# One ScalarE instruction for the square roots of two places, with GpSimd's pieces in the first

## The reference

```python
q2 = jnp.sum(q * q, axis=-1)
k2 = jnp.sum(k * k, axis=-1)
qk = jnp.einsum('bhid,bhjd->bhij', q, k)
d2 = jnp.maximum(q2[..., :, None] + k2[..., None, :] - 2.0 * qk, 1e-12)
attn = jax.nn.softmax(-jnp.sqrt(d2), axis=-1)
out = jnp.einsum('bhij,bhjd->bhid', attn, v)
```

## Time and profile before

| | us |
|---|---|
| median of three runs | 1473.09 |
| the profiled execution | 1471.27 |
| its span, first to last instruction | 1469.5 |
| ScalarE busy | 1431.2 (97%) |
| VectorE busy | 1224.0 (83%) |
| TensorE matmul busy | 1119.0 (76%) |
| GpSimd busy | 833.3 (57%) |
| exponentials of layer 0 (L830), 63 | 438.9 |
| roots of layer 0 in whole places (L791), 59 | 388.1 |
| exponentials of layer 1 (L1349), 438 | 432.6 |

### The profile page before, as it was taken

The page is one execution under the profiler, slowest core; times in us unless marked ns, Lnnn a source line. Parts: engine busy times, 40 slices in busy tenths (PEclk is TensorE's granted clock), DMA queues, the critical chain, the costliest instruction groups (busy, mean ns, idle before and its releaser), DMA issues.

```text
span 1469.5 us, 22500 instructions
## 1 busy us (share of the span) xinstructions
PE 1119.0 (76%) x8231; PEld 471.7 (32%) x8260; DVE 1224.0 (83%) x2196; ACT 1431.2 (97%) x796; POOL 833.3 (57%) x737
## 2 busy tenths in 40 slices
PE   5588786887887988879878784787777677776766
PEld 2133234253452552534515321232223122221212
DVE  6988978978979779779697799858898898997886
ACT  3999999999999999999999999999999999999998
POOL 5178899768778787797887885633213033023100
PEclk8588988999999989899899997899999999999999
DMA  4942644222232234254352521033033033021020
GB/s 118 251 134 65 175 130 127 53 58 75 77 89 66 63 105 140 69 155 112 90 157 57 129 69 30 20 120 82 27 127 70 27 113 82 29 103 33 27 70 16
DMA packets 113185, 130.04 MB, mean 88 GB/s; under 512 B 42906, under 2 KB 81178, under 8 KB 113066
## 3 DMA queue, kind: packets, MB, share of 16 engines
q1 hardware_dynamic: 107738, 116.74, 29.0%
q0 software_dynamic: 4464, 11.09, 2.8%
q10 hardware_dynamic: 864, 0.69, 0.2%
HBM read 83.79 MB, written 44.70 MB: 87 GB/s over the span
## 4 chain that ended last, share of the span: by engine, by line
ACT 29%; PE 24%; DVE 23%; issue 17%; POOL 4%; DMA 1%; SPq 1%; DVEq 0%; ACTq 0%; POOLq 0%
DVE scores L737 15%; ACT exp L1349 11%; PE pvb L718 8%; ACT scores L830 8%; ACT scores L791 7%; PE ring L703 5%; PE ring L1059 5%; DVE exp L1357 4%; PE ring L1070 3%; ACT exp L1345 2%; POOL yro L1136 1%; PE ring L1324 1%; PE ring L480 1%; DMA w<-in_w 1%; ACT L830 0%
## 5 line engine op out<-in xcount | busy, mean ns | idle before, releaser
L737 DVE TENSOR_SCALAR scores<-ring 128x1024 f32<-128x1024 f32 x512 | 588.7, 1212 | 14.9 <-PE ring L703 14.7
L830 ACT ACTIVATE scores<-scores 128x8192 f32<-128x8192 f32 x63 | 438.9, 7021 | 0.2
L1349 ACT ACTIVATE exp<-ring 128x1024 f32<-128x1024 f32 x438 | 432.6, 1418 | 0.2
L1324 PE MATMUL ring<-stk 128*128 128x512 bf16 x995 | 299.9, 385 | 127.9 <-ACT exp L1349 106.2
L791 ACT ACTIVATE scores<-scores 128x7296 f32<-128x7296 f32 (+2 forms) x59 | 388.1, 6641 | 8.1 <-DVE scores L737 7.9
L1357 DVE SCALAR_TENSOR_TENSOR exp<-exp 128x512 f32<-128x512 f32 x438 | 322.2, 757 | 62.5 <-ACT exp L1349 58.2
L718 PE MATMUL pvb<-scores,val 128*9 128x256 f32 x4096 | 325.6, 393 | 61.4 <-issue 34.2
L703 PE MATMUL ring<-stk 64*128 64x512 bf16 x1024 | 210.2, 408 | 67.5 <-DVE scores L737 56.7
L1324 PEld LDWEIGHTS ring<-stk 128*128 128x128 bf16 x1024 | 65.8, 97 | 337.9 <-ACT exp L1349 241.7
L703 PEld LDWEIGHTS ring<-stk 64*128 64x128 bf16 x1024 | 49.8, 93 | 303.2 <-DVE scores L737 215.3
L718 PEld LDWEIGHTS pvb<-scores,val 128*9 128x9 f32 x4096 | 65.3, 89 | 184.8 <-issue 181.1
(11 more groups left out here) (263 smaller groups left out, 1482.0 us busy)
## 6 DMA issues: line engine op xcount, KB each, us to landing
stk<-stack SPq DMA_DIRECT2D x192, 192.0 KB, 2.9
w<-in_w SPq DMA_DIRECT2D x39, 352.0 KB, 3.4
w<-in_w SPq DMA_DIRECT2D x39, 192.0 KB, 2.9
stack<-qp SPq DMA_DIRECT2D x7, 768.0 KB, 4.4
stack<-kp SPq DMA_DIRECT2D x7, 768.0 KB, 5.7
xj<-xg SPq DMA_DIRECT2D x10, 448.0 KB, 4.7
yg<-xj POOLq DMA_DIRECT2D x10, 448.0 KB, 3.7
stack<-qp SPq DMA_DIRECT2D x7, 512.0 KB, 5.1
```

Source lines behind the costliest of these rows:

```text
L737: nc.vector.tensor_scalar(S[place][:, j * N:(j + 1) * N], tile, 1e-12, None, ALU.max).then_inc(o.release(("qk", group, place, j)), 1)
L830: nc.scalar.activation(S[place][:], S[place][:], ACT.Exp, scale=-1.0).then_inc(exp_done, 1)
L1324: mm = nc.tensor.matmul(out[:, cols], stk1[place][:, Q, i * P:(i + 1) * P], stk1[place][:, K, cols], start=True, stop=True)
L1349: nc.scalar.activation(EX[k // 2][:, k % 2, :], tile, ACT.Exp, scale=SCALE1).then_inc(o.release(("qk1", n, i)), 1)
```

## The change

- The tiles of places 0 and 1 are allocated as one tile `S01` of 16384 columns; `S[0]` and `S[1]` are its halves.
- From round 3 on (`PAIRED_FROM`), ScalarE takes the roots of places 0 and 1 by one instruction, over the columns of `S01` from the end of place 0's pieces to the end of place 1. It waits for the last chunk of place 1, and counts `root_done` up by 2.
- From round 3 on, GpSimd's pieces of place 1 are pieces of place 0, in the same widths.

```diff
-    ((), (896,), (448, 448), (448,)),
-    ((), (896,), (), ()),
-    ((), (448, 448), (), ()),
-    ((), (896,), (448, 448), ()),
...
-    ((), (448, 448), (448, 448), ()),
-    ((), (448, 448), (448,), ()),
+    ((896,), (), (448, 448), (448,)),
+    ((896,), (), (), ()),
+    ((448, 448), (), (), ()),
+    ((896,), (), (448, 448), ()),
...
+    ((448, 448), (), (448, 448), ()),
+    ((448, 448), (), (448,), ()),
 ]
...
-        S = [scores(f"scores{i}", [P, CH * N]) for i in range(GROUP - 1)]
+        S01 = scores("scores01", [P, 2 * CH * N])
+        S = [S01[:, 0:CH * N], S01[:, CH * N:2 * CH * N], scores("scores2", [P, CH * N])]
...
+        def act_root_pair(act, o, group):
+
+            o.emptied(act, ("qk", group, 1, CH - 1))
+            part = S01[:, columns_by_pool(group, 0):2 * CH * N]
+            nc.scalar.activation(part, part, ACT.Sqrt).then_inc(root_done, 2)
...
+        PAIRED_FROM = FIRST_JOBS
...
-                        for place in range(GROUP):
+                        if r >= PAIRED_FROM:
+                            act_root_pair(act, o, r)
+                        for place in range(2 if r >= PAIRED_FROM else 0, GROUP):
                             act_root_halves(act, o, r, place) if (r, place) == (1, GROUP - 1) else act_root(act, o, r, place)
...
                         for place in range(1, GROUP - 1):
-                            pool_roots(pool, o, roots, r, 1, place - 1, place)
+                            pool_roots(pool, o, roots, r, 0, place - 1, place)
...
                     if r > 1 and r != PLACE_ROUND + 1:
-                        pool_roots(pool, o, roots, r, 1)
+                        pool_roots(pool, o, roots, r, 1 if r < PAIRED_FROM else 0)
```

## The result

The changed kernel takes 1478.18 us (median of 15 runs, 1474.55 to 1480.70), the kernel before 1474.69 (15 runs, 1472.44 to 1476.42). The ratio is 1.0025, 95% interval 1.0018 to 1.0033: 3.7 us slower, with an interval from 2.7 to 4.9. The median of the kernel before over 15 runs is itself 1.6 us above that of the three runs of the prediction. The profiled execution of the changed kernel took 1480.70 us, the slowest of its 15.

What follows compares the result with a forecast made beforehand. ScalarE, busy 97% of the span, was taken as the bound. Round 4's +0.43, rounds 5 to 15's 11 x -0.096 = -1.06 and round 3's 0 gave -0.63 us: 1472.5 us from a 1473.09 median, range 1469.5 to 1475.8.

Steps and rivals of the forecast that it cites:

- Added: First root waits for place 1's last tile instead of place 0's; only round 4 late, by 4.19 us, costing 0.43 us.
- rival (a): ScalarE's wait stands ahead of the table load, which no longer hides it: +1.5 us, 1474.6 us; chance 0.10.
- a root with one wait like the pair: Evidence against the wait preceding the load: at 29.78 ScalarE loaded the table, then its first root stood 5.03 us.
- 0.43+1.28: Round 4 if the wait precedes the load: late pair's 0.43 us plus 1.28 us of load, +1.71 us.
- The joint: Cost between two back-to-back ScalarE roots, saved by the long root: 0.096 us a round, bounds 0 and 0.204.
- met by the 1.7 us that ScalarE is then behind: Round 13 if the wait precedes the load: ScalarE's lag covers the missing margin, so no added cost.
- +0.22: Round 14 if the wait precedes the load: 1.28 us needed against a margin of 1.06, adding 0.22 us.
- +0.65 less 0.10: Round 15 if the wait precedes the load: adds 0.65 us; the saved instruction is worth 0.096 us a round.
- the 6.65 us of cover: Round 4: GpSimd's piece ends at 302.65, exponential 0 starts at 309.30, so the new need costs nothing.
- the 0.11 us from mark to root: A stalled ScalarE root starts 0.11 us after VectorE's mark of a place's end; used to work out margins.
- the length of the long root: ScalarE's joined root in rounds 3 to 15: 128x15488, at some 13.1 us.
- the +5.7 us: Wait ahead of the load, with the skill's 1380 ns drain also behind it: +5.7 us, 1478.8 us; chance 0.01.

Runs made afterwards that it cites:

- one count: Changed kernel with the pair adding one to root_done instead of two, exponentials' waits adjusted: 1474.05 us, ratio 0.9999 to the kernel before.
- two counts: Kernel before, roots still single, but place 0's root adds two to root_done from round 3 on: 1473.01 us, ratio 0.9997.
- the two late roots: Changed kernel with two roots in place of the long one, both behind place 1, one count each: 1473.75 us, ratio 1.0003 to the kernel before.
- the pair with later gathers: Changed kernel with root_done raised by one per pair and round 14's gathers moved behind GpSimd's root pieces: 1471.99 us, ratio 0.9992 to the kernel before.

## Why the prediction was wrong

**The step that failed: "Added".** The prediction took the margin of a pair against the start of the root. That holds only if the load stands ahead of the wait. It gave rival (a) 0.10 because of the earlier trace rows, a root with one wait like the pair. The two differ in what they signal: that root signals nothing, the pair counts two. With a count of two the wait became an instruction of its own, and the table load was put between it and the root; with one count, the wait stayed on the root. The diff showed the two, and no root of the kernel before counts by two. The row was the wrong analogue, and the chance too small.

**The size of rival (a), +1.5 us for 3.7.** Its steps against the runs:

- Round 4: the step 0.43+1.28 = +1.71; measured 28.44-26.67 = +1.77. Rival (a) had this step right.
- The joint: 0.096 us a round; measured 0.09. The 13 long roots average 13.12 us, as forecast.
- Round 13: forecast 0, "met by the 1.7 us that ScalarE is then behind". Measured: a round of 59.85 us (load of round 12 to load of round 13) against 58.68 before, +1.2. The marks of place 1 are not independent of ScalarE there. In rounds 7 to 9 they stand 4.47 us ahead of the root in the kernels before and after alike, as TensorE is released by ScalarE's first exponential; so ScalarE's lag of round 4 had passed into the marks, and only the slack shrinks from there to round 13. The margin of the earlier trace rows was 1.19 us, under 1.28 by itself, and the joints of rounds 10 to 13 bring ScalarE 0.4 us nearer. The chain from place 1 of round 9 to that of round 13 also took 238.7 us in both profiles of the changed kernel; it took 237.9 and 237.7 in the two of the kernel before, and 238.7 in that with two counts, so this part belongs to the execution and not to the change. From the mark of round 9 to the end of round 13's exponentials the changed kernel takes 295.1 us in both profiles, and the one-count kernel and the two profiles of the kernel before 294.3.
- Round 14: forecast +0.22, since the row had place 1 ready 1.06 us ahead. Where round 14 is unpaired and the hole stands in place 1, three profiles have it 2 to 4 us late for place 0's root. Behind the mark of place 1 the roots then end 898.34-871.67 = 26.67 us later, in the one-count kernel too; in the changed kernel 902.60-874.92 = 27.68: +1.0 for the load.
- Round 15: forecast +0.65 less 0.10; measured, from one load for the exponentials to the next, 57.74-57.10 = +0.6.

With round 13's +1.2, round 14's +1.0 and round 15's +0.6, less 8 x 0.09 for rounds 5 to 12, the sum is +3.9 us against the 3.7 measured. The steps come from one or two profiles each, so the nearness of the sums is in part luck.

**What stays open: TensorE ahead of round 14.** In the second profile of the changed kernel TensorE waits 2.33 us before its first value product of round 14, and then its granted clock falls to the lower of its two levels (near 0.5 of 2.4 GHz) for some 3 us. Place 0 of round 14 ends 20.50 us behind ScalarE's load for the exponentials of round 13. The rows, and the stretch behind the wait (us; busy of PE, PEld, DVE, ACT, POOL; granted clock; DMA share; GB/s):

```profile
846.95 0.62 PE L719 MATMUL pvb<-scores,val 128*9 128x256 f32 x8 [2.33 <-ACT scores L837]
```

```profile
849.00:852.00 3.00, 3.00 (x26) 0.58 (x28) 2.60 (x4) 3.00 (x1) 2.71 (x3) 0.56 0.00 0
```

The kernel before with two counts waits 1.49 us, keeps its clock, and place 0 ends 18.53 us behind that load:

```profile
845.53 0.62 PE L718 MATMUL pvb<-scores,val 128*9 128x256 f32 x8 [1.49 <-ACT scores L830]
```

```profile
848.00:851.00 3.00, 3.00 (x39) 0.76 (x38) 3.00 (x3) 3.00 (x1) 2.75 (x4) 1.00 0.00 0
```

These two alone suggest that the late pair of round 13 caused the longer wait. But the kernel before has the wait and the fall of the clock in both of its own profiles, where no pair is late: 2.85 us in the earlier trace rows, and in the second profile 3.12 us, with place 0 ending 858.39-837.52 = 20.87 us behind the load:

```profile
845.99 1.04 PE L718 MATMUL pvb<-scores,val 128*9 128x256 f32 x8 [3.12 <-ACT scores L830]
```

```profile
846.00:849.00 3.00, 3.00 (x20) 0.46 (x20) 1.22 (x1) 3.00 (x1) 2.75 (x5) 0.50 0.02 5
```

Nine of the fourteen profiles have such a fall there, with and without pairs. That it costs the changed kernel anything beside the others is not shown, and no run changed that wait alone.

**What held.** No exponential waits for GpSimd in the profile after, as the 6.65 us of cover promised. The value of a joint, the 0.11 us from mark to root, the length of the long root, and the 0.42 us of a late pair in round 4 came out as worked. With the wait behind the load the change is worth what the forecast said, nothing that can be measured: 0.9999 (0.9990 to 1.0008) for a forecast of 0.9996. That agreement is weak, since the interval holds no change at all just as well. The prediction's test for rival (a), a gap ahead of the load in rounds 14 and 15, was met. In all five late rounds the pair follows the start of its 1.28 us load after 1.29 or 1.30 us. The Trainium skill (ScalarE: Activation LUTs, section "What ACT_TABLE_LOAD costs") adds a drain of 1380 ns to each load; the trace does not agree, and the +5.7 us that the prediction estimated from it did not come.

**The level.** The span of 1469.5 us was taken for the kernel's ordinary run. It was the one profile without the hole of round 14, and its execution took 1.7 to 2.3 us less than the medians of the later groups; the prediction noted 1.8 us against its own median and asked no further. The range was built on four executions from 1471.27 to 1476.42, all of the kernel before, and so had no room for a rival of its own above its price.

## What to carry to other kernels

Ask of each edited instruction which instruction will carry its wait, and read that from the built program and not from a neighbour: here a count of two moved a wait ahead of a 1.28 us table load. It costs nothing as long as the wait is over in time, and up to the whole load where it isn't, so a change that delays a release should keep the load ahead of it (one count, or a small instruction of the same table). And take the margins from more than one profile: the first one of the kernel before lacked a stall that all the others have. Its time alone did not give that away, since the profiled executions of the two late roots and of the pair with later gathers also took 1.8 to 2.0 us less than their medians, and have the stall.

## What the runs showed of the hardware

- Joining two roots of 7296 and 8192 columns saves 0.09 us, not the fixed 0.20 of an instruction; the rate holds up to 15488 columns (13.12 us, which is 0.833 us per 1000 columns and 0.2 fixed).
- While GpSimd's eight indirect gathers run, or just behind them, VectorE and TensorE stand still, in most profiles with no releaser in the records. In 13 of the 14 profiles the place in question takes 2.8 to 4.6 us more than its 9.75. The hole moved with the gathers from place 1 to place 3 in all three kernels that moved them. What it is that the gathers hold up is open.
- A late pair costs less than its lateness: with one count it was 4.25 us late in round 4 and cost 0.42 us at the end of the roots, since VectorE brings a place only every 9.75 us.
